# Graph layer with residual and norm on one core: x's part of the update moved behind the products for the edge tables, for seven of thirteen groups instead of three

## The chip, the cores and the metric

The kernel runs on one core of a Trainium2 chip. The metric is the device time of one execution in microseconds; of several runs the median is given.

## The reference

6250 nodes with 128 features each, and 100,000 edges that are sorted by their target node. A message goes through three layers, the messages of a node are averaged, and the node is updated and normalised:

```python
msg_in = jnp.concatenate([x[src], x[dst]], axis=-1)      # 100000 x 256
h = relu(msg_in @ Wm1 + bm1)                             # 256 x 256
h = relu(h @ Wm2 + bm2)                                  # 256 x 256
messages = h @ Wm3 + bm3                                 # 256 x 128
agg = segment_sum(messages, dst) / clip(count, 1)        # 6250 x 128
upd = relu(concatenate([x, agg], -1) @ Wn1 + bn1) @ Wn2 + bn2
out = layernorm(x + (x + upd))
```

## The kernel before

The kernel has three stages. The first works over nodes, in 13 groups of four tiles of 128 nodes (the last group has one tile). For each group it loads x, transposes it on TensorE, and splits the transposed values into a rounded high part (copied by ScalarE, L678) and the rest, the low part (VectorE, L965). With these it computes three products. The product A is x times the upper half of Wm1, and it goes with the bias through `a_out` to the DRAM table `a_table` (L1271 on TensorE, L979 on VectorE, store L508). The product B is x times the lower half of Wm1, and it goes as high part (ScalarE, L662) and low part (VectorE, L989) through `b_out` to `b_table` (store L512). The third product is x's part of the last layer, x times the upper half of Wn1 (`x_product`, L1234); ScalarE copies it with the bias bn1 to `hx` (L669), where it stays until the end. Each of the three takes three terms, high by high, high by low and low by high.

The second stage is the loop over 391 blocks of 256 edges. GpSimd gathers rows of `a_table` by source node (L630), SyncE loads a window of `b_table` (L543) and the target nodes relative to it (`rel`, L546), VectorE makes one-hot matrices (L1023, L1038), TensorE transposes the gathered rows (L1413), adds the expanded window (L1324), computes the second layer (L1437) and sums over the target nodes (L1341 to L1349). ScalarE and VectorE make the high and the low parts of both layers' results (L732, L1106, L740, L1118). The third stage takes the means through the last layers and the norm, group by group.

Each engine has its own program, written out by hand, and they wait for each other by semaphores. In round `g` of the first stage TensorE transposes group `g`, computes the x product that stands first in that round's list `x_groups(g)`, then A of group `g - 1`, then B of the groups `b_groups(g)`, and then the second of `x_groups(g)`, if there is one. B follows one group behind, but B of groups 11 and 12 both stand in the last round, 13. Round 13 also holds the product of Wm3 and the lower half of Wn1 (transposes L1283, copy L865 on VectorE, products L1290 and L1292).

The parts of x lie in seven buffers (`x_parts`, seven being `XB`), which are slices of tensors that the second stage uses: h2_lo, h2_hi, h1, onehot and, for group 6, b_win, the target of SyncE's window loads. wna, the weight of the x product, lies in `onehot_t`. VectorE makes the first `onehot_t` only after `s_bits`, which TensorE's matmul at L1301 raises behind all x products, and after clearing a bank (L1001). `a_out` has two buffers. `b_out` has three, the third of which lies in `a_edge`, where the gathers go; from group 9 on only the first two are used (`b_at`), and a copy into one waits for the store of its last use. The x products use two pairs of banks, (2, 3) and (6, 7); an x product waits for ScalarE's copies of an earlier one:

```python
                if k in X_LAST[1:]:
                    pe.wait_ge(s_hxa, 2 * (x_nth(k) - 2))
                elif k:
                    pe.wait_ge(s_hxa, 2 * (x_nth(k) - 1))
```

In the kernel before, the x products stand as follows: groups 0 and 1 in round 5, 2 in round 6, 3 in round 7, 4 and 5 in round 8, 6 to 9 in rounds 9 to 12 (one each), and 12, 11 and 10 in round 13: the short one of group 12 ahead of L1290, the two others behind it. Ahead of its loop SyncE waits for all stores of both tables and for the words of all blocks (`s_rw`); ScalarE waits for all of its own copies to `hx`.

Of the kernel before, what the change touches and what calls it, by code (L numbers as in the profile page):

```python
# [25 lines left out]
XB = 7  # L26
XA = 5
# [7 lines left out]
def gnn_layer(nc, x, src, dst, Wm1, bm1, Wm2, bm2, Wm3, bm3, Wn1, bn1, Wn2, bn2, out):  # L35
# [13 lines left out]
    NG = -(-NW // GW)  # L49
# [11 lines left out]
    with ExitStack() as ctx:  # L61
# [3 lines left out]
        def sem(name):  # L65
            return ctx.enter_context(nc.semaphore(name))
# [189 lines left out]
        s_hx = sem("s_hx_product")  # L256
# [49 lines left out]
        def size(g):  # L306

            return min(GW, NW - g * GW) if 0 <= g < NG else 0
# [23 lines left out]
            return [NG - 2, NG - 1] if g == NG else [g - 1] if 1 <= g < NG - 1 else []  # L332


        TWICE = (XA, XA + 3)

        def x_groups(g):

            done = max(g - XA, 0) + sum(XA <= t < g for t in TWICE)
            return list(range(done, NG if g == NG else min(done + 1 + (g in TWICE), NG))) if g >= XA else []  # L340

        X_LAST = [NG - 1, NG - 2, NG - 3]
        assert x_groups(NG) == sorted(X_LAST) and all(g >= XB + x for x in range(NG - 3) for g in (XB + x,)
                                                      if x not in x_groups(g))
        X_ORDER = [k for k in range(NG - 3)] + X_LAST

        def x_banks(k):
            return (2, 3) if k == NG - 2 else (6, 7)  # L350

        def x_nth(k):

            return X_ORDER.index(k) + 1

# [6 lines left out]
        def b_uses(k, g):  # L362

            return sum(b_at(j) == k for j in range(g))
# [96 lines left out]
        def _(sp):  # L461
# [43 lines left out]
            for g in range(1, NG + 1):  # L505
                k = g - 1
# [26 lines left out]
            for k in range(3):  # L533
                sp.wait_ge(s_bs[k], 16 * b_uses(k, NG))
            sp.wait_ge(s_rw, 11)

            def body(i):
                first = load_words(sp, words_sp, i * U, U, PAD_DST)
                for k in range(U):
                    if there(i, k - RB):  # L540
                        sp.wait_ge(s_ex, i * U + (k - RB + 1))
                    if there(i, k):
                        sp.dma_start(b_win[:, k % RB, :].bitcast(F32),  # L543
                                     b_table[bass.ds(first[k] * 2, P), :]).then_inc(s_bw[k % RB], 16)
                    if k % 2 == 1:
                        sp.dma_start(rel[:, k // 2, :].rearrange("p (b e) -> p b e", b=2),  # L546
                                     rel_dram[bass.ds(i * U + (k - 1), 2), :].partition_broadcast(P)
                                     ).then_inc(s_rc[k // 2], 16)
# [90 lines left out]
        def _(act):  # L639
# [25 lines left out]
            def copy_hx(k):  # L665
                n = size(k)
                act.wait_ge(s_hx, x_nth(k))
                for h, to in enumerate((hx[0], hx_more)):
                    act.activation(to[:, k * GW * P:(k * GW + n) * P], bank[x_banks(k)[h]][:, 0:n * P],  # L669
                                   ACT.Identity, bias=bn1_col[:, h:h + 1]).then_inc(s_hxa, 1)  # L670

            for g in range(NG + 1):
# [25 lines left out]
                if g < NG:  # L698
                    for k in x_groups(g)[1:2]:
                        copy_hx(k)  # L700
            for k in X_LAST:
                copy_hx(k)
# [499 lines left out]
        def _(pe):  # L1202
# [21 lines left out]
            def x_product(k):  # L1224

                n = size(k)
# [5 lines that stand above are left out]
                for h in range(KH):  # L1232
                    for n_, (xp, a) in enumerate(((0, 0), (0, 1), (1, 0))):
                        ins = pe.matmul(in_pairs(bank[x_banks(k)[h]], n), wna[:, a, h * P:(h + 1) * P], x_part(k, xp),  # L1234
                                        start=(n_ == 0), stop=(n_ == 2))
                ins.then_inc(s_hx, 1)

            for g in range(NG + 1):

                if g == 4:  # L1240
                    pe.wait_ge(s_efs, 1)
                    edge_transposes(0)
                if g == 7:
                    pe.wait_ge(s_hxa, 2 * x_groups(g)[0])
                    pe.wait_ge(s_rel, 1)
                    edge_transposes(1)
                n, k = size(g), g % 2
                if n:
                    pe.wait_ge(s_x[g], 16)
                    if g >= 2:  # L1250
                        pe.wait_ge(s_xl, g - 1)
                    for j in range(n):
                        ins = pe.transpose(bank[k][:, j * P:(j + 1) * P], f_x[:, g * GW + j, :], ident[:, :])
                    ins.then_inc(s_xt, 1)
                if g < NG:
                    for k in x_groups(g)[0:1]:
                        if k == 0:
                            pe.wait_ge(s_wnas, 1)
                            pe.wait_ge(s_ec, GR)
                        if g == 7:  # L1260
                            pe.wait_ge(s_ec, 2 * GR)
                        x_product(k)
                if g == 1:
                    pe.wait_ge(s_split, 1)
                n, k = size(g - 1), g - 1
                if n:
                    pe.wait_ge(s_xl, g)
                for q in range((n + 1) // 2):
                    if k >= 1:
                        pe.wait_ge(s_ac, pair(k - 1, q))  # L1270
                    products(bank[2 + q], k, q, 0).then_inc(s_pa, 1)  # L1271
                for k in b_groups(g):
                    for q in range((size(k) + 1) // 2):
                        if k >= 1:
                            pe.wait_ge(s_bl, pair(k - 1, q))
                        products(bank[4 + q], k, q, 1).then_inc(s_pb, 1)
                if g < NG:
                    for k in x_groups(g)[1:2]:
                        x_product(k)
                if g == NG:  # L1280
                    pe.wait_ge(s_w3, 48)
                    for c in range(KH):
                        ins = pe.transpose(bank[0][:, c * P:(c + 1) * P], w3[:, c, :], ident[:, :])  # L1283
                    ins.then_inc(s_w3t, 1)
                    x_product(X_LAST[0])

                    pe.wait_ge(s_ac, NPAIR)
                    pe.wait_ge(s_w3c, 1)
                    for c in range(KH):
                        pe.matmul(bank[1][:, c * H:(c + 1) * H], w3_t[:, c * P:(c + 1) * P], wn1[:, 1, :],  # L1290
                                  start=True, stop=True)
                    pe.matmul(bank[0][0:2, H:2 * H], b3_col[:, :], wn1[:, 1, :], start=True, stop=True  # L1292
                              ).then_inc(s_wcp, 1)
                    x_product(X_LAST[1])
                    x_product(X_LAST[2])

            pe.wait_ge(s_bl, NPAIR)
            pe.wait_ge(s_const, 8)
# [153 lines left out]
            for g in range(NG + 2):  # L1452
                n, k = size(g), g % 2
# [60 lines left out]
```

## Time and profile before

| | |
|---|---|
| runs | 1200.52, 1201.52, 1202.63 us; median 1201.52 us |
| the profiled execution | 1202.17 us, span from first to last instruction 1200.4 us |
| TensorE | busy 1168.4 us, 97% of the span; mean granted clock 0.992 of full |
| VectorE, ScalarE, GpSimd | busy 966.4, 747.2, 773.9 us |
| first block of the second stage on TensorE | from 89.83 us |

Times in the trace count from the first instruction. In the rows below PE is TensorE's matmul, DVE VectorE, ACT ScalarE, POOL GpSimd, and SPq the instructions by which SyncE issues transfers. A line L1234 is that of the kernel's file. The busy times are no measure of what bounds a stage: matmuls are pipelined, and their ends are modelled. The 1.77 us between the span and the execution's time lie outside the instructions.

### The profile page before, as it was taken

Reading aid. Unit: us, or ns where it says so; the run is one execution under the profiler, and the core shown is the slowest. Engines: PE = TensorE matmul, PEld = TensorE weight load, DVE = VectorE, ACT = ScalarE, POOL = GpSimd, SP = SyncE. Lnnn points to the kernel's source line nnn. Section 1 sums busy time; section 2 is a strip of 40 time slices with the busy share of each in tenths; the row PEclk is TensorE's granted clock in tenths of the full one; section 3 lists DMA queues with packets and bytes.
Section 4 is the critical chain, followed back from the end, with each engine's and each line's share of the span. In section 5 each row is a group of like instructions: output and inputs, shape, how many; then the busy total and the mean of one; then the engine's idle time right before and its main releaser. Section 6 shows DMA issues by size and latency. Waiting matters only on the chain.

```text
span 1200.4 us, 33956 instructions
## 1 busy us (share of the span) xinstructions
PE 1168.4 (97%) x9614; PEld 1147.6 (96%) x9615; DVE 966.4 (81%) x2072; ACT 747.2 (62%) x1392; POOL 773.9 (64%) x814
## 2 busy tenths in 40 slices
PE   6879999999999999999999999999999999999996
PEld 6769999999999999999999999999999999999886
DVE  6766888888777888788888888888888888987676
ACT  3545666666666666666666666666666666664684
POOL 2067777777777777777777777777777777771000
PEclk9999999999999999999999999999999999999998
DMA  9776666666666666665666666666666666662022
GB/s 328 277 284 181 179 179 177 180 179 175 182 180 177 179 178 178 179 183 178 176 178 180 177 181 178 175 179 180 177 181 176 179 176 180 178 178 73 27 71 92
DMA packets 135605, 211.42 MB, mean 176 GB/s; under 512 B 24247, under 2 KB 102669, under 8 KB 134030
## 3 DMA queue, kind: packets, MB, share of 16 engines
q0 software_dynamic: 37536, 102.55, 31.2%
q1 hardware_dynamic: 98030, 108.43, 29.3%
q8 instruction: 14, 0.23, 0.1%
q14 instruction: 25, 0.20, 0.1%
HBM read 188.09 MB, written 22.80 MB: 176 GB/s over the span
## 4 chain that ended last, share of the span: by engine, by line
PE 93%; DVE 2%; SPq 1%; DMA 1%; issue 1%; ACT 1%; POOL 0%; ACTq 0%; DVEq 0%
PE bank L1437 46%; PE bank L1413 14%; PE bank L1324 8%; PE sums L1347 4%; PE sums L1341 4%; PE sums L1345 4%; PE sums L1349 4%; PE bank L1478 3%; PE sums L1491 2%; PE bank L1234 1%; PE bank L1219 1%; PE sums L1219 1%; PE bank L1461 1%; PE bank L1474 0%; PE sums L1462 0%
## 5 line engine op out<-in xcount | busy, mean ns | idle before, releaser
L630 POOL DMA_INDIRECT a_edge<-a_table,src_idx x782 | 754.5, 965 | 255.0 <-issue 176.8
L1437 PE MATMUL bank<-w,h 128*128 128x256 f32 x4692 | 618.8, 281 | 0.0
L1437 PEld LDWEIGHTS bank<-w,h 128*128 128x128 f32 x4692 | 582.5, 189 | 0.0
L732 ACT ACTIVATE h<-bank 128x512 fp32r<-128x512 f32 x391 | 233.9, 598 | 321.2 <-PE bank L1324 319.9
L1106 DVE SCALAR_TENSOR_TENSOR h<-bank,h 128x512 fp32r<-128x512 f32 x391 | 269.3, 689 | 125.3 <-ACT h L732 91.8
L1118 DVE SCALAR_TENSOR_TENSOR h_lo<-bank,h_hi 128x512 fp32r<-128x512 f32 x391 | 266.5, 682 | 0.0
L721 ACT COPY bank<-b_bc 128x512 f32<-128x512 f32 x391 | 231.6, 592 | 46.9 <-DVE h_lo L1118 42.9
L1413 PE MATMUL bank<-ident,a_edge 128*128 128x128 f32 x1564 | 235.8, 273 | 7.0 <-DVE onehot_t L1023 5.6
L740 ACT ACTIVATE h_hi<-bank 128x512 fp32r<-128x512 f32 x391 | 232.9, 596 | 2.9 <-PE bank L1437 2.9
L1324 PE MATMUL bank<-onehot_t,b_win 128*128 128x256 f32 x782 | 189.9, 324 | 0.0
L1413 PEld LDWEIGHTS bank<-ident,a_edge 128*128 128x128 f32 x1564 | 181.2, 140 | 8.1 <-DVE onehot_t L1023 6.7
L1023 DVE TENSOR_SCALAR onehot_t<-rel,node_half 128x256 fp32r<-128x256 int16 x391 | 149.1, 382 | 49.0 <-DMA rel<-rel_dram 36.5
L1038 DVE SCALAR_TENSOR_TENSOR onehot<-iota,first_node,dst_col 128x256 fp32r<-128x256 int16 x391 | 186.1, 476 | 0.5 <-PE sums L1349 0.5
L1324 PEld LDWEIGHTS bank<-onehot_t,b_win 128*128 128x128 f32 x782 | 118.8, 192 | 0.3 <-issue 0.3
L1341 PE MATMUL sums<-h_hi,onehot 128*128 128x258 f32 x391 | 111.0, 284 | 0.2
L1347 PE MATMUL sums<-h_hi,onehot 128*128 128x258 f32 x391 | 111.0, 284 | 0.0
L1345 PE MATMUL sums<-h_lo,onehot 128*128 128x256 f32 x391 | 110.2, 282 | 0.1
L1349 PE MATMUL sums<-h_lo,onehot 128*128 128x256 f32 x391 | 109.9, 281 | 0.0
L1341 PEld LDWEIGHTS sums<-h_hi,onehot 128*128 128x128 f32 x391 | 73.6, 188 | 0.9 <-issue 0.8
L1345 PEld LDWEIGHTS sums<-h_lo,onehot 128*128 128x128 f32 x391 | 74.0, 189 | 0.5 <-issue 0.4
L1347 PEld LDWEIGHTS sums<-h_hi,onehot 128*128 128x128 f32 x391 | 74.1, 189 | 0.0
L1349 PEld LDWEIGHTS sums<-h_lo,onehot 128*128 128x128 f32 x391 | 73.5, 188 | 0.0
(190 smaller groups left out, 681.1 us busy)
## 6 DMA issues: line engine op xcount, KB each, us to landing
b_win<-b_table SPq DMA_DIRECT2D x391, 128.0 KB
rel<-rel_dram SPq DMA_DIRECT2D x196, 128.0 KB, 3.3
a_edge<-a_table,src_idx POOLq DMA_INDIRECT x782
a_table<-work SPq DMA_DIRECT2D x12, 512.0 KB, 4.4
b_table<-work SPq DMA_DIRECT2D x5, 1024.0 KB, 5.7
b_table<-h SPq DMA_DIRECT2D x4, 1024.0 KB, 5.3
f_x<-in_x SPq DMA_DIRECT2D x12, 256.0 KB, 4.5
b_table<-a_edge SPq DMA_DIRECT2D x3, 1024.0 KB, 5.6
```

The source lines that it names most:

```text
L630: pool.indirect_dma_start(a_edge[:, b % R * TB + t, :], None, a_table, bass.IndirectOffsetOnAxis(ap=src_idx[:, b * TB + t:b * TB + t + 1], ...
L721: act.copy(bank[H2[k % U]][:, :], b2_bc[:, :, :].rearrange("p t h -> p (t h)")).then_inc(s_bias, 1)
L732: act.activation(h1[:, k % U, 0, :], bank[k % 2][:, :], ACT.Relu).then_inc(s_h1h, 1)
L740: act.activation(h2_hi[:, (k - LAG) % U, :, 0:H], bank[H2[(k - LAG) % U]][:, :].rearrange("p (t h) -> p t h", t=TB), ACT.Relu).then_inc(s_ ...
L1106: dve.scalar_tensor_tensor(h1[:, k % U, 1, :], bank[k % 2][:, :], 0.0, h1[:, k % U, 0, :].bitcast(F32), ALU.max, ALU.subtract).then_inc(s_ ...
L1118: dve.scalar_tensor_tensor(h2_lo[:, j, :, :], bank[H2[j]][:, :].rearrange("p (t h) -> p t h", t=TB), 0.0, h2_hi[:, j, :, 0:H].bitcast(F32) ...
L1324: ins = pe.matmul(bank[k % 2][:, h * EB:(h + 1) * EB], rows[:, h * P:(h + 1) * P], hot, start=False, stop=True, skip_group_check=True)
L1341: return pe.matmul(to[:, 0:HC], onehot[:, slot, 0, :], h2_hi[:, k % U, 0, :], start=start, stop=False, skip_group_check=True)
L1345: pe.matmul(to[:, 0:H], onehot[:, slot, 0, :], h2_lo[:, k % U, 0, :], start=False, stop=False, skip_group_check=True)
L1347: pe.matmul(to[:, 0:HC], onehot[:, slot, 1, :], h2_hi[:, k % U, 1, :], start=False, stop=False, skip_group_check=True)
L1413: ins = pe.matmul(bank[k % 2][:, h * EB + t * P:h * EB + (t + 1) * P], a_edge[:, k % R * TB + t, h * P:(h + 1) * P], ident[:, :], start=(t ...
L1437: ins = pe.matmul(to, h1[:, j, a, h * EB + t * P:h * EB + (t + 1) * P], w2[:, b, h, :], start=False, stop=(a == 1 and h == KH - 1), skip_g ...
```

## The change

The list of x products is made anew. Groups 0 and 1 stand in round 5 and groups 2 to 5 in rounds 6 to 9, one each; rounds 10 to 12 have none; groups 6 to 12 all stand in round 13, in this order: 6 ahead of L1290, 7 to 12 behind it, on the two pairs of banks in turn. Since the parts of group 6 lie in b_win, SyncE waits for that group's product ahead of its loop.

```diff
-        TWICE = (XA, XA + 3)
+        X_LAST = list(range(NG - XB, NG))
 
         def x_groups(g):
 
-            done = max(g - XA, 0) + sum(XA <= t < g for t in TWICE)
-            return list(range(done, NG if g == NG else min(done + 1 + (g in TWICE), NG))) if g >= XA else []
-
-
-
-        X_LAST = [NG - 1, NG - 2, NG - 3]
-        assert x_groups(NG) == sorted(X_LAST) and all(g >= XB + x for x in range(NG - 3) for g in (XB + x,)
-                                                      if x not in x_groups(g))
-        X_ORDER = [k for k in range(NG - 3)] + X_LAST
+            first = [[0, 1], [2], [3], [4], [5]]
+            return X_LAST if g == NG else first[g - XA] if XA <= g < XA + len(first) else []
+
+        X_ORDER = [k for g in range(NG + 1) for k in x_groups(g)]
+        assert X_ORDER == list(range(NG)) and all(k + XB > g for g in range(NG) for k in x_groups(g))
 
         def x_banks(k):
-            return (2, 3) if k == NG - 2 else (6, 7)
+            return (2, 3) if k in X_LAST[1::2] else (6, 7)
@@ SyncE, ahead of its loop
             sp.wait_ge(s_rw, 11)
+            sp.wait_ge(s_hx, x_nth(max(k for k in range(NG) if k % XB == XB - 1)))
@@ TensorE, at the end of round NG
-                    x_product(X_LAST[1])
-                    x_product(X_LAST[2])
+                    for k in X_LAST[1:]:
+                        x_product(k)
```

## Rows read from the trace of the kernel before

**Rows 1.** The page, busy time of each engine, its share of the span and instructions.

```profile
PE 1168.4 (97%) x9614; PEld 1147.6 (96%) x9615; DVE 966.4 (81%) x2072; ACT 747.2 (62%) x1392; POOL 773.9 (64%) x814
```

**Rows 2.** The chain of waits that ended last: start us, us, what.

```profile
79.28 3.75 DMA b_table<-h
...
109.26 3.00 issue
```

**Rows 3.** Timeline of TensorE: start us, us, instruction, count, [idle before, releaser].

```profile
17.05 2.90 PE L1219 MATMUL bank<-h,h_hi 128*128 128x256 f32 x12 [2.48 <-DVE work L979]
...
30.25 2.90 PE L1234 MATMUL bank<-h_lo,onehot_t 128*128 128x512 f32 x6 [3.35 <-DVE onehot_t L969]
...
46.35 1.66 PE L1234 MATMUL bank<-h_hi,onehot_t 128*128 128x512 f32 x6 [1.59 <-ACT dst_col L646]
...
78.36 0.86 PE L1234 MATMUL bank<-onehot,onehot_t 128*128 128x128 f32 x6
79.73 1.10 PE L1290 MATMUL bank<-work 128*128 128x256 f32 x4 [0.51 <-DVE work L865]
...
81.28 1.65 PE L1234 MATMUL bank<-h,onehot_t 128*128 128x512 f32 x6
...
84.20 0.39 PE L1301 MATMUL sums<-w,ones 128*128 128x512 f32 x1
89.83 1.12 PE L1413 MATMUL bank<-ident,a_edge 128*128 128x128 f32 x4 [5.24 <-DVE onehot_t L1023]
90.60 0.78 PE L1324 MATMUL bank<-onehot_t,b_win 128*128 128x256 f32 x2
...
98.26 0.60 PE L1413 MATMUL bank<-ident,a_edge 128*128 128x128 f32 x4
98.62 0.48 PE L1324 MATMUL bank<-onehot_t,b_win 128*128 128x256 f32 x2
```

**Rows 4.** Timeline of VectorE.

```profile
84.88 0.48 DVE L1001 MEMSET sums<- 128x512 f32 x1 [0.34 <-PE sums L1301]
89.42 0.73 DVE L1023 TENSOR_SCALAR onehot_t<-rel,node_half 128x256 fp32r<-128x256 int16 x2 [4.06 <-DMA rel<-rel_dram]
...
102.04 0.35 DVE L1023 TENSOR_SCALAR onehot_t<-rel,node_half 128x256 fp32r<-128x256 int16 x1 [1.23 <-DMA a_edge<-a_table,src_idx]
```

**Rows 5.** Windows: length; busy us (instructions) of PE, PEld, DVE, ACT, POOL; PEclk, DMA share, GB/s.

```profile
55.00:69.20 14.20, 13.28 (x91) 11.93 (x91) 14.13 (x26) 8.65 (x16) 3.42 (x1) 1.00 0.63 256
65.00:78.00 13.00, 12.15 (x90) 11.26 (x89) 9.95 (x18) 7.43 (x14) 10.89 (x1) 1.00 0.97 394
...
90.00:94.50 4.50, 4.11 (x19) 3.81 (x20) 2.06 (x5) 2.17 (x4) 2.28 (x4) 0.50 0.52 158
96.00:98.00 2.00, 2.00 (x19) 2.00 (x19) 0.35 (x1) 0.95 (x2) 1.39 (x3) 1.00 0.63 210
```

**Rows 6.** Timeline of ScalarE.

```profile
78.42 0.37 ACT L662 CAST h<-sums 128x256 fp32r<-128x256 f32 x1 [0.73 <-PE sums L1219]
...
84.41 0.69 ACT L669 ACTIVATE f_x<-bank,bn_col 128x512 f32<-128x512 f32 x1 [0.16 <-PE bank L1234]
84.99 0.68 ACT L669 ACTIVATE work<-bank,bn_col 128x512 f32<-128x512 f32 x1
86.81 0.59 ACT L721 COPY bank<-b_bc 128x512 f32<-128x512 f32 x1 [1.14 <-issue]
```

**Rows 7.** Timeline of SyncE: issues of A(10)'s and B(10)'s stores.

```profile
71.29 0.33 SPq L508 DMA_DIRECT2D a_table<-work  x1
73.34 0.33 SPq L512 DMA_DIRECT2D b_table<-h  x1
```

**Rows 8.** The same stores, DMA issues 70:72 and 72:75: count, KB, us to landing.

```profile
a_table<-work SPq DMA_DIRECT2D x1, 512.0 KB, 4.3
...
b_table<-h SPq DMA_DIRECT2D x1, 1024.0 KB, 4.7
```

**Rows 9.** Timeline of GpSimd: the gather for block 4.

```profile
91.65 0.94 POOL L630 DMA_INDIRECT a_edge<-a_table,src_idx  x1 [1.61 <-PE bank L1324]
```

## The prediction

> **What bounds the kernel now.** I read the page first: TensorE has 97% of the span as busy time [rows 1], most of it in the loop over edge blocks. The change touches nothing there, so it can only move the moment at which that loop gets going, and all that follows with it. So I read the stretch ahead of it. The chain of waits shows what set its end: the last store of b_table is issued at 79.28 and lands 3.75 us later, at 83.03 [rows 2]; then come SyncE's loads for the first blocks, VectorE waits 4.06 us for rel and makes the first onehot_t at 89.42, and TensorE starts block 0 at 89.83 after 5.24 us of idleness [rows 3, 4]. In that idle time the change has its room.
>
> Why did the last store not leave earlier? The windows give two answers. From 55.0 to 69.2 VectorE is busy 14.13 of 14.20 us: it has its row arithmetic (first words, whole words, flags) besides the copies of A and the low parts of B. From 65 to 78 the DMA engines are at a share of 0.97 and move 394 GB/s [rows 5]. TensorE is busy in both stretches too, but it isn't alone, and the other two keep their work.
>
> **What the change takes away ahead of the stores.** Names: x(k) is the product of x's part for group k; A(k), B(k) are that group's products for the two tables; rounds are the loop's steps. x(0) to x(4) stay where they are. x(5) goes from the end of round 8 to round 9; x(6) to x(9) leave rounds 9 to 12. A full x product costs TensorE 1.46 us (two of them between 81.28 and 84.20 [rows 3]), so 5.8 us leave TensorE before the last B, and on ScalarE four pairs of copies at 1.26 (84.41 to 85.67 [rows 6]). What does this give the stores? Up to 69.2 nothing: VectorE's 14.13 us stay, so the stores of groups 8 and 9 are issued when they were, and TensorE waits instead. After that the issues of A(10), B(10), A(11), B(11) can come one to two us earlier, but they come into a queue that is full. A(10) lands at 71.29 + 4.3 = 75.6, B(10) at 73.34 + 4.7 = 78.0 [rows 7, 8]: 2.4 us for its 1024 KB, 437 GB/s. From there to 83.03 the rest lands, 512 + 128 + 1024 + 256 KB in 5.0 us, 394 GB/s. At 437 throughout it would be 4.5 us. So the end of the stores can gain about 0.5 us, and no more as long as the queue decides.
>
> There is a second tie. From group 9 on B has two staging buffers (`b_at`), so ScalarE's copy of B(12) waits for the store of B(10). It ran at 78.42 [rows 6], 0.4 us after that store landed at 78.0. It can therefore come at 78.05, a gain of 0.37. VectorE's low part and its copy of w3's transpose follow in order, and TensorE's w3 product (L1290) starts 1.31 us after ScalarE's copy (78.42 to 79.73 [rows 3, 6]): 79.36 now. B(12) itself doesn't bind here: VectorE's copy of A(12), which stands ahead of the low parts of B(11) in its program, waits for the store of A(10), landed at 75.6; then the two low parts of B(11) (0.69 us each at most, an estimate from ScalarE's copies of that shape [rows 6]), and B(12) is done by 77.3. x(6) fits between B(12) and L1290: 77.4 to 78.9 with the two transposes of w3.
>
> **What the change puts behind.** Behind L1290 stood x(11) and x(10); now there stand x(7) to x(11) and the short x(12), which before ran ahead of L1290. The first starts 1.55 us after L1290 (79.73 to 81.28). Their pace: TensorE could do 1.46, but with two pairs of banks a product waits for the copies of the one two before it; a product's row is 1.65 us, and the pair of copies behind it is 1.26, so two products can't follow in less than 2.91, and each semaphore between the engines adds a little. I take 1.50 each; the bounds are 1.46 (TensorE alone) and 1.65 (the whole row of one product, no overlap at all between neighbours). x(12) costs 0.8, from its row of 0.86 less its overlap with the next. So the marker matmul L1301, which all of VectorE's loop waits for, starts at 79.36 + 1.55 + 5 x 1.50 + 0.8 = 89.2, against 84.20: 5.0 later. VectorE had waited 4.06 us for rel after the memset that this matmul releases. That cover is used up: rel, if it follows the stores, lands 0.5 earlier, at 88.9, while the memset now ends at 90.4. So the first onehot_t is 5.0 - 4.06 = 0.95 later, and TensorE starts block 0 at 90.8, not 89.83.
>
> **What the start gives back.** After its 5.24 us of idleness TensorE ran the first steps at a granted clock of 0.50 from 90.0 to 94.5, that is 1.2 GHz, and at 1.00, 2.4 GHz, from 96 to 98 [rows 5]. Block 0, transposes and expansion, took from 89.83 to 91.38, 1.55 us; block 4 at full clock from 98.26 to 99.10, 0.84 [rows 3]. Now TensorE works until 89.6 and idles some 1.2 us. Idleness of 1.59 us before 46.35 left an x product at 1.66 us, of 3.35 us before 30.25 made it 2.90, and of 2.48 us before 17.05 left twelve A products at 2.90 [rows 3], so at 1.2 us I take the full clock. Block 0 is then expanded at 90.8 + 0.84 = 91.6, against 91.38: 0.2 later. This is the moment that counts, because GpSimd's gather for block 4 waits for it (91.65 after 1.61 idle [rows 9]) and from there gathers follow without a gap, and VectorE waits for them until block 6 and later (1.23 us at 102.04 [rows 4]).
>
> ScalarE is later by more. Its last copies end near 90.6, and 1.14 us of issue stand between them and put_b2, as at 86.81 [rows 6]; so its first relu comes near 92.2, not 91.4, and block 2's transposes with it 0.8 later. Two blocks at half clock with the first h2 product had taken TensorE some 1.2 us more than at full clock, so by block 3 this is paid back. The new wait of SyncE for x(6), near 79, stands behind its wait for the last store, past 82, and costs nothing; behind it stand only the loads of b_win. ScalarE's own waits and GpSimd's queue keep their order; nothing is moved past them, and no DMA is added or dropped.
>
> **The sum** is +0.2 us: 0.37 gained at the stores, 5.38 us of work put behind L1290, 4.06 of cover, 0.7 back at the clock. Against the profiled execution's 1202.17 (span 1200.4) it is 1202.4; the median of the runs, 1201.52, lies 0.65 below that execution, so I say 1201.7. Bounds of the terms: stores -0.5 to +0.3, pace of five products -0.2 to +0.75, clock 0 to +0.7.
>
> **Rivals.**
> (a) *The stores land sooner.* If a store's time were its own and not the queue's, B(10), issued near 71.7 instead of 73.34, would land at 75.5 in the 3.75 us of the last store [rows 2], which had little behind it; then B(12) on TensorE binds, 77.3, L1290 comes at 78.6, and the sum is -0.55: 1201.0. For it: the issues do come earlier. Against it: the landings follow each other at the queue's rate. The Trainium skill (DMA: Bandwidth & Descriptors, Anatomy of one DMA) gives a DMA about 2.0 us plus its bytes at 436 GB/s, which for this store would be an estimated 4.4 us and a landing at 76.1, much as in this rival. By it the sum would be -0.55 too. The trace doesn't agree for this store, which took 4.7 us [rows 8]; by that row the sum stays at +0.2.
> (b) *The loop still starts at 1.2 GHz*, since the first steps have waits between them (1.2 us ahead of block 0, then for the late relu): the 0.7 isn't given back, +0.9: 1202.4. For it: from 90 to 94.5 the clock stayed low though TensorE was busy 4.11 of 4.50 us.
> (c) *Slower: TensorE drops to 1.2 GHz ahead of the tail.* With x(6) to x(9) gone it waits for VectorE and for stores between 60 and 77, by my estimate up to 2.9 us in round 10 (the two products that leave rounds 9 and 10, 2 x 1.46) and up to 2 us ahead of B(12), which waits until the store of A(10) has landed at 75.6. Idleness of 2.48 us was enough at 17.05, of 1.59 was not at 46.35. If it falls ahead of B(12), x(6) takes 2.9 us [rows 3] instead of 1.5, and B(12) and the transposes, by the same ratio, 0.5 more; L1290 comes 1.85 later, and the sum is +2.05; if the loop's start is slow as well, +2.75: 1204.3. It decides from a fall that costs x(6) and block 0 together. A fall in round 10 alone costs nothing, since VectorE is behind then.
> (d) *Faster by more*: the 3.00 us of issue at 109.26 in the chain [rows 2], ScalarE's on entering the loop, goes when ScalarE comes there from other waits. Nothing in the rows ties it to the change; -3: 1198.7.
>
> **How the numbers follow.** The sum as it stands 55%, (a) 14%, (b) 13%, (c) 12%, (d) 6%. A measurement of this kernel can tell about 0.2%, 2.4 us, from no change. The first three cases lie within that; half of (c) and a rest of unforeseen costs lie above it, (d) and a rest of unforeseen gains below: faster 0.09, same 0.75, slower 0.16. The runs shown lie 2.1 us apart, so a median can be off by 1. The likeliest case's own range is 1200.5 to 1203.2; with the bounds of the terms and most of (c), 1199.4 to 1204.6.
>
> **What would show it.** Right: in the changed profile VectorE stays full from 55 to 69 and the stores land back to back, the last near 82.5; L1290 near 79.4, five long x products behind it at 1.5, L1301 near 89.2; VectorE's first onehot_t waits for TensorE and not for rel; block 0 begins near 90.8 at granted clock 1.00. Wrong: the last store landing before 81.5, products at over 1.7, a granted clock of 0.5 in the tail, or ScalarE's first relu, not the gathers, setting the pace beyond block 4.

## The result, and the profile after

The changed kernel takes 1203.62 us (median of 20 runs, 1201.26 to 1205.86), the kernel before 1202.12 us in as many runs beside it (1200.03 to 1204.57). The ratio is 1.0013, its 95% interval 1.0007 to 1.0019: 0.8 to 2.3 us slower, 1.5 in the middle. The prediction had said +0.2 us and "same" by a bound of 0.2%, and a range that holds the time; the sign of its sum was right, its size was not. That the sign came out right says little, since by its own bounds for the terms the sum could also have been below zero. Where the other 1.3 us come from is the question of this study.

The profiled execution took 1205.11 us with a span of 1203.3. Its page, busy time of each engine, answers to [rows 1]:

```profile
PE 1168.0 (97%) x9614; PEld 1147.2 (95%) x9615; DVE 960.7 (80%) x2072; ACT 748.3 (62%) x1392; POOL 772.1 (64%) x814
```

The sums of work are as they were; only the order moved. What lies ahead of the change shifts everything behind it by up to 2.4 us from profile to profile, so times are counted from one instruction that the change doesn't reach: VectorE's operation over the words of all blocks. VectorE works without a gap for 8.2 us up to it, in before (from 50.82) as in after (from 52.20). In the profile of before and in that of after (timeline of VectorE) it stands at

```profile
59.04 0.55 DVE L925 CUSTOM_DVE_ANT_0 words_pe<-words_pe,agg 1x784 uint16<-1x784 uint16 x1
```

```profile
60.41 0.55 DVE L922 CUSTOM_DVE_ANT_0 words_pe<-words_pe,agg 1x784 uint16<-1x784 uint16 x1
```

so 1.37 is subtracted from a time of after to compare it with one of before. Of these 1.37 us 1.1 arise in round 5, ahead of the change, where the two profiles run the same instructions. TensorE's granted clock from 30 to 38 us was 0.79 in before and 0.59 in after, and the twelve products of an A and of a B took longer; first before's, then after's:

```profile
32.95 1.95 PE L1219 MATMUL bank<-h 128*128 128x256 f32 x12
34.74 1.60 PE L1219 MATMUL sums<-h 128*128 128x256 f32 x12
```

```profile
33.27 2.76 PE L1216 MATMUL bank<-h 128*128 128x256 f32 x12
35.83 1.89 PE L1216 MATMUL sums<-h 128*128 128x256 f32 x12
```

Times counted from the words operation leave this out, but the time of an execution holds it. Lines of after are 3 or 4 lower: L1287 is before's L1290, L1298 its L1301, L1020 its L1023. TensorE's timeline of after, answering to [rows 3]:

```profile
64.81 2.90 PE L1216 MATMUL bank<-h,h_hi 128*128 128x256 f32 x12 [2.98 <-DVE work L976]
...
78.82 0.63 PE L1216 MATMUL sums<-h,onehot 128*128 128x256 f32 x3 [0.69 <-DVE work L986]
79.28 0.38 PE L1280 MATMUL bank<-ident,work 128*128 128x128 f32 x2
79.42 1.63 PE L1231 MATMUL bank<-b_win,onehot_t 128*128 128x512 f32 x6
80.89 1.02 PE L1287 MATMUL bank<-work 128*128 128x256 f32 x4
...
82.36 3.03 PE L1231 MATMUL bank<-h_lo,onehot_t 128*128 128x512 f32 x12
85.37 3.06 PE L1231 MATMUL bank<-h_hi,onehot_t 128*128 128x512 f32 x12
88.40 1.66 PE L1231 MATMUL bank<-h,onehot_t 128*128 128x512 f32 x6
89.90 0.78 PE L1231 MATMUL bank<-onehot,onehot_t 128*128 128x128 f32 x6
90.52 0.44 PE L1298 MATMUL sums<-w,ones 128*128 128x512 f32 x1
92.75 0.66 PE L1410 MATMUL bank<-ident,a_edge 128*128 128x128 f32 x4 [1.79 <-DVE onehot_t L1020]
93.17 0.48 PE L1321 MATMUL bank<-onehot_t,b_win 128*128 128x256 f32 x2
```

The reader is to see the moved products there: x(6) at 79.42, x(7) to x(11) from 82.36 to 89.90 at 1.5 us each, x(12), and the marker matmul at 90.52, which is 89.15 in before's time (89.2 was predicted). VectorE, answering to [rows 4], and the chain of waits in that place, which shows what VectorE's sequencer does between its two instructions:

```profile
91.25 0.48 DVE L998 MEMSET sums<- 128x512 f32 x1 [5.52 <-PE sums L1298]
92.34 0.61 DVE L1020 TENSOR_SCALAR onehot_t<-rel,node_half 128x256 fp32r<-128x256 int16 x2 [0.61 <-issue]
```

```profile
82.44 8.25 PE bank L1231 x36
90.68 0.29 PE sums L1298
...
91.60 0.59 DVEq L418
...
92.34 0.36 DVE onehot_t L1020
...
92.75 0.33 PE bank L1410
...
113.48 2.92 issue
```

From round 10 to block 0 no DMA stands in this chain. The wait of 4.06 us for rel is gone, but 0.61 us of "issue" remain between the memset and the first onehot_t: mostly L418, VectorE's loads of the first blocks' words into registers. Before, they ran under the wait for rel and no row showed them. The last line is the 3 us of issue on entering the loop [rows 2], still there, now found on VectorE.

GpSimd's gather for block 4, answering to [rows 9], and the windows, answering to [rows 5] (the last one, 64 to 66, is new):

```profile
93.92 0.95 POOL L627 DMA_INDIRECT a_edge<-a_table,src_idx  x1 [2.37 <-PE bank L1321]
```

```profile
55.00:69.20 14.20, 11.22 (x75) 10.75 (x74) 13.65 (x26) 5.16 (x10) 2.04 (x1) 0.81 0.64 259
65.00:78.00 13.00, 12.25 (x80) 12.00 (x80) 10.17 (x18) 3.65 (x7) 10.84 (x1) 0.78 0.85 343
90.00:94.50 4.50, 2.54 (x20) 2.02 (x18) 1.28 (x4) 3.19 (x7) 1.83 (x3) 1.00 0.52 164
96.00:98.00 2.00, 2.00 (x19) 2.00 (x19) 0.96 (x3) 0.60 (x1) 1.39 (x3) 1.00 0.62 195
64.00:66.00 2.00, 1.19 (x5) 1.22 (x6) 2.00 (x5) 0.00 (x0) 0.00 (x0) 0.50 0.00 0
```

The first two show that VectorE stays full up to 69 (13.65 of 14.20 us) while TensorE falls behind it, and that the DMA engines are less full from 65 to 78 than in before (0.85 and not 0.97). The last shows that TensorE's clock is at 0.50 (1.2 GHz) around the products that follow the idleness of 2.98 us in round 10. The third shows the loop's start at 1.00 (2.4 GHz), where before had 0.50.

Counted from the words operation, the steps stand like this (a subtraction of rows, 59.04 and 60.41):

| | before | after | difference |
|---|---|---|---|
| w3 product (L1290, now L1287) | 20.69 | 20.48 | -0.21 |
| marker matmul (L1301, now L1298) | 25.16 | 30.11 | +4.95 |
| block 0 on TensorE | 30.79 | 32.34 | +1.55 |
| gather for block 4 | 32.61 | 33.51 | +0.90 |

### The profile page after: what moved, and what is told of

It reads as the page before. It is cut to its first block, busy times and chain, and to the rows that moved or that the text cites. A ratio compares the mean times of both kernels' runs of the same rounds, so it can differ in the third digit from the quotient of the medians.

```text
span 1203.3 us, 33956 instructions
## 1 busy us (share of the span) xinstructions
PE 1168.0 (97%) x9614; PEld 1147.2 (95%) x9615; DVE 960.7 (80%) x2072; ACT 748.3 (62%) x1392; POOL 772.1 (64%) x814
## 4 chain that ended last, share of the span: by engine, by line
PE 93%; DVE 3%; DMA 1%; issue 1%; POOL 1%; ACT 0%; SPq 0%; DVEq 0%
PE bank L1434 45%; PE bank L1410 14%; PE bank L1321 8%; PE sums L1344 4%; PE sums L1338 4%; PE sums L1342 4%; PE sums L1346 4%; PE bank L1475 3%; PE sums L1488 2%; PE bank L1231 1%; PE bank L1458 1%; PE bank L1216 1%; PE sums L1216 1%; POOL a_edge L627 1%; PE bank L1471 0%
## 5 line engine op out<-in xcount | busy, mean ns | idle before, releaser
L1020 DVE TENSOR_SCALAR onehot_t<-rel,node_half 128x256 fp32r<-128x256 int16 x391 | 144.1, 369 | 54.0 <-DMA rel<-rel_dram 40.7
```

## The experiments

The expectations use letters. **T**: the start of the loop is held by the products behind L1287, less what VectorE's wait for rel had covered, and the gathers of the first blocks carry the delay on. **C**: the cost is the clock's fall in round 10. **F**: the rounds ahead of L1287, from which x products were taken, give back or cost a part of it. **Q**: the last stores are bound by a full DMA queue. **L**: the loads behind the last stores still hold the start. Each kernel was timed in five rounds, beside the kernel before on the same chip.

**One part of the cover taken away in the kernel before** (`e1_rel_three`): SyncE loads rel for the first blocks ahead of its wait for the last stores.

```diff
@@ SyncE, ahead of the wait for the stores; the loop then skips these loads for i = 0
+            sp.wait_ge(s_rw, 11)
+            first_of_0 = load_words(sp, words_sp, 0, U, PAD_DST)
+            for c in range(RC):
+                load_rel(2 * c, c)
```

> The kernel before, with SyncE's loads of rel for the first four blocks, and its registers for their windows, ahead of its wait for the last stores. Theory T (ahead of the change the start of the edge loop was set by the loads that follow the last store, which cover TensorE's tail; the change puts 5.4 us of x products behind L1290 and uses that cover up): block 0 on TensorE starts near 87 instead of 89.8, and from there GpSimd's gathers, which idled 1.6 us ahead of block 4, hold it: 1.0 to 1.6 us faster than before. If the loads behind the last store held nothing, no change.

1201.76 us against 1202.36, ratio 0.9998 (0.9988 to 1.0008). Block 0 came at 29.55 behind the words operation, 1.24 earlier than in before, and the gather for block 4 at 32.19, 0.42 earlier. The 1.0 to 1.6 us that were expected did not come, and no gain is shown. Block 0 did not come near 87 either: with rel there, VectorE's first onehot_t waits for another load behind the stores, SyncE's window of b_table, which has to stay behind them, since it reads what they write:

```profile
88.53 0.57 DVE L1030 TENSOR_SCALAR onehot_t<-rel,node_half 128x256 fp32r<-128x256 int16 x1 [2.18 <-DMA b_win<-b_table]
```

What else holds the gather for block 4 a kernel below shows.

**The same in the changed kernel** (`e2_rel_seven`).

> The changed kernel with the same two moves on SyncE. Theory T: TensorE's tail holds the start, so earlier loads give nothing: 1.0 to 2.0 us slower than the kernel before, as the changed kernel is, and VectorE's first onehot_t comes behind L1298 as there. Rival L (the loads behind the last stores still hold the start, and the changed kernel's loss is elsewhere): it gains 1 us or more over the changed kernel.

1203.86 us, ratio 1.0010 (1.0001 to 1.0019); block 0 at 32.53. With seven groups behind, the loads are not what block 0 waits for. This profile bears on C as well: behind the same 2.98 us of idleness in round 10 the clock stayed at 1.00 from 64 to 66, and block 0 came as late as in after.

```profile
64.53 1.66 PE L1223 MATMUL bank<-h,h_hi 128*128 128x256 f32 x12 [2.98 <-DVE work L983]
```

**The tail cut short** (`e3_short_tail`): in the changed kernel only the high by high term is computed for groups 7 to 12; the two other terms are left out.

```diff
-                    for n_, (xp, a) in enumerate(((0, 0), (0, 1), (1, 0))):
+                    terms = ((0, 0),) if k > X_LAST[0] else ((0, 0), (0, 1), (1, 0))
+                    for n_, (xp, a) in enumerate(terms):
```

> The changed kernel with one term of three (high by high) in the x products of groups 7 to 12: two thirds of that product's work are left out. Theory T: the tail shrinks to ScalarE's pace of 1.26 us a group, L1298 comes some 2 us earlier than in the changed kernel, the loads of rel hold the start again, and the time is within 0.5 us of the kernel before. Rival C (the cost is the drop of TensorE to 1.2 GHz in round 10, and the late B(9)): it stays 1.0 to 2.0 us slower than before.

1201.85 us, ratio 1.0001 (0.9993 to 1.0010): the cost is gone, while all other instructions of the change, those of rounds 9 to 12 included, are in place. The clock did not fall in round 10 in this profile, so it alone doesn't speak against C; it fell in the tail instead, to 0.50 from 86 to 88. VectorE's timeline:

```profile
88.37 0.48 DVE L998 MEMSET sums<- 128x512 f32 x1 [3.63 <-PE sums L1299]
89.46 0.61 DVE L1020 TENSOR_SCALAR onehot_t<-rel,node_half 128x256 fp32r<-128x256 int16 x2 [0.61 <-DMA rel<-rel_dram]
```

The trace names rel here as what ended the wait, but onehot_t follows the memset by the same 0.61 us as in after: that is the least they stand apart.

**Five and six groups behind** (`e7_five`, `e8_six`): in the changed kernel groups 6 and 7, or 6 alone, go back to rounds 10 and 11.

```diff
-        X_LAST = list(range(NG - XB, NG))
+        X_LAST = list(range(NG - 5, NG))       # e8: NG - 6
-            first = [[0, 1], [2], [3], [4], [5]]
+            first = [[0, 1], [2], [3], [4], [5], [6], [7]]      # e8: without [7]
```

> Five products behind (groups 8 to 12; 6 and 7 go back to rounds 10 and 11), so three full ones and the short one behind L1290 instead of five and the short one. Theory T: the tail ends before the loads behind the last store, which set the start again: within 0.5 us of the kernel before, VectorE's first onehot_t waits for a DMA. Rival C (TensorE's idleness in front is what costs): between the two kernels, about 0.8 us slower than before.

> Six products behind (groups 7 to 12; 6 goes back to round 10): four full ones and the short one behind L1290. Theory T: the tail and the loads end within 0.5 us of each other, block 0 starts up to 0.5 us later than in the kernel before but at the full clock, so -0.5 to +0.7 us. Rival C: about 1.2 us slower than before.

1201.71 us (1.0001, 0.9992 to 1.0010) and 1202.61 us (1.0004, 0.9995 to 1.0013). Block 0 is at 30.31 and 32.28. With five behind the cover holds: the first onehot_t still waits 1.29 us for rel. With six it doesn't in this profile, but the tail was not all that came late there. TensorE's clock fell ahead of it, behind 1.58 and 1.88 us of idleness:

```profile
78.00:82.00 4.00, 4.00 (x14) 2.38 (x12) 1.08 (x4) 1.64 (x3) 1.13 (x1) 0.61 0.87 350
```

The marker matmul came 30.04 behind the words operation, no earlier than in after with one product more (30.11). With after's rows behind the w3 product and four long products in place of five, an estimate for block 0 is 30.9, beside 30.79 in before. So six stand at the edge of the cover, and its time is not shown to be above before's.

**The clock kept up** (`e4_warm`): ten dummy matmuls into a bank that is free then, in round 10 of the changed kernel.

```diff
+                if g == 10:
+                    pe.wait_ge(s_hxa, 2 * x_nth(5))
+                    for _ in range(10):
+                        pe.matmul(bank[6][:, :], wab[:, 0, 0:P], wab[:, 0, :], start=True, stop=True)
```

> The changed kernel with ten extra matmuls of 512 columns into a free bank in round 10, in the gap of 3 us in which TensorE waits for VectorE; their result isn't used. Theory T: the clock stays at 2.4 GHz, the store of B(9) is issued 1 to 1.6 us earlier, but the stores land as before in the changed kernel, and the time stays 1.0 to 2.0 us slower than the kernel before. Rival C: the loss goes, within 0.5 us of the kernel before.

1205.42 us (7 runs), ratio 1.0027 (1.0016 to 1.0038). TensorE's timeline shows that the dummies did what they were for, since A(9) takes 1.67 us and not 2.90:

```profile
61.79 2.54 PE L1265 MATMUL bank<-h 128*128 128x512 f32 x10
65.02 1.67 PE L1216 MATMUL bank<-h,h_hi 128*128 128x256 f32 x12 [0.68 <-DVE work L976]
```

The w3 product didn't come sooner for it (20.61 behind the words operation, 20.48 in after), and the time is no shorter. With e2, where the clock stayed up without dummies and block 0 came no sooner, C is excluded as the cost. That this kernel is slower than the changed one was not expected; it was run again below.

**The tail without the rest of the change** (`e5_twice_three`): the kernel before, with the products of groups 7 to 10 computed a second time behind the three, into the sum banks that the memset clears; their results are not used.

```diff
@@ TensorE, behind x_product(X_LAST[2])
+                    pe.wait_ge(s_bl, NPAIR)
+                    for k in (7, 8, 9, 10):
+                        for h in range(KH):
+                            for n_, (xp, a) in enumerate(((0, 0), (0, 1), (1, 0))):
+                                pe.matmul(in_pairs(bank[SUM + h], GW), wna[:, a, h * P:(h + 1) * P], x_part(k, xp),
+                                          start=(n_ == 0), stop=(n_ == 2))
```

> The kernel before with four x products (groups 7 to 10) computed once more behind the last one, into the two sum banks, where nothing reads them: the tail of the changed kernel with nothing taken away in front. Theory T: 5.8 us on TensorE against a cover of 3.4 us (4.06 us of waiting less VectorE's 0.6 us of register loads, which the wait had hidden): block 0 starts 2.4 us later but at the full clock, and the time is 1.4 to 2.4 us above the kernel before, hardly more than in the changed kernel, since moving the products gave the stores only 0.2 to 0.4 us. Rival F (the moved products do free the front, and the tail costs more than the net shows): 3 us or more above the kernel before.

1205.47 us against 1201.83, ratio 1.0028 (1.0018 to 1.0038). That the tail alone makes before slower is shown, but +3.4 us is above T's bound and in F's. By place it isn't F: the w3 product starts at 20.70 here, as in before (20.69), and in the changed kernel at 20.48 in one profile and 20.80 in another, so taking the products away ahead of it gained nothing there. Block 0 at 32.88 is 0.54 later than in after, and 0.16 later than in the second profile of the changed kernel. What the rest of +3.4 is stays open.

**VectorE's register loads moved ahead** (`e6_setup_seven`): in the changed kernel they stand ahead of the wait for the marker matmul.

```diff
-            dve.wait_ge(s_bits, 1)
-            dve.memset(bank[SUM][:, :], 0.0).then_inc(s_sz, 1)
@@ behind VectorE's other preparations for the loop
+            words_of_0 = load_words(dve, words_dve, 0, words_of(0, BACK + 2), DVE_TOP)
+            dve.wait_ge(s_bits, 1)
+            dve.memset(bank[SUM][:, :], 0.0).then_inc(s_sz, 1)
```

> The changed kernel with VectorE's register setup and its loads of the first words ahead of its wait for TensorE's marker matmul L1298. Theory T: VectorE's first onehot_t follows its memset at once, block 0 starts 0.6 to 0.9 us earlier than in the changed kernel, and the time is 0.3 to 1.2 us above the kernel before. If that setup isn't on the path, no change from the changed kernel, 1.0 to 2.0 us above.

1204.17 us, ratio 1.0016 (1.0007 to 1.0025). The 0.6 us are real: VectorE's onehot_t follows its memset at once, and block 0 and the gather for block 4 come 0.71 earlier than in after (31.63 and 32.80). The time didn't follow: it was expected at 0.3 to 1.2 us above before, and a gain of 0.7 on the changed kernel is neither shown nor excluded by intervals of this width. In this profile TensorE's clock fell behind block 2 instead:

```profile
91.05 0.48 DVE L1012 MEMSET sums<- 128x512 f32 x1 [5.36 <-PE sums L1300]
91.44 0.54 DVE L1021 TENSOR_SCALAR onehot_t<-rel,node_half 128x256 fp32r<-128x256 int16 x2
```

```profile
95.32 0.66 PE L1412 MATMUL bank<-ident,a_edge 128*128 128x128 f32 x4 [1.94 <-DVE onehot_t L1021]
95.73 0.48 PE L1323 MATMUL bank<-onehot_t,b_win 128*128 128x256 f32 x2
96.05 2.36 PE L1436 MATMUL bank<-w,h 128*128 128x256 f32 x12
98.21 1.05 PE L1412 MATMUL bank<-ident,a_edge 128*128 128x128 f32 x4
```

**Both covers taken away in the kernel before** (`e9_rel_setup_three`): the edits of the first and of the last experiment together, with three groups behind.

> The kernel before (three groups behind) with both covers taken away: SyncE issues the first five loads of rel ahead of its wait for the last stores, and VectorE loads the first words into registers ahead of its wait for the marker matmul. Theory T (the start is held by the last marker matmul, then by the gathers of the fill, which run on GpSimd from the landing of the last store of a_table): block 0 comes 1.0 to 1.8 us earlier than before, but the gather of block 4 only 0.0 to 0.4 us earlier, counted from the words operation; the time is 0.3 to 1.2 us below before. If GpSimd's chain of gathers is the whole limit, the time is within 0.5 us of before, as with the loads of rel alone (-0.6).

1200.68 us against 1202.01, ratio 0.9994 (0.9985 to 1.0003): the lowest median of the study, but not shown to be faster. Block 0 is at 29.09, 1.70 earlier than in before, the gather for block 4 at 31.70, 0.91 earlier, more than expected. The chain of waits shows the next limit:

```profile
76.42 3.46 DMA a_table<-work
79.89 0.52 issue
80.41 1.13 POOL a_edge L637
...
89.54 0.95 POOL a_edge L637
90.48 0.30 issue
90.79 0.95 POOL a_edge L637
```

From the landing of a_table's last store GpSimd issues the gathers of the first blocks, most of them 1.25 us apart, and the one for block 4 (90.79) comes 10.38 us behind the first (80.41) without a gap. In before that distance was 11.50 (80.15 to 91.65), in after 12.44 (81.48 to 93.92), with the first loads of rel alone 10.39 (81.40 to 91.79). So, with a_table's last store landing when it does, 1.1 us is all that an earlier start could give to before, and these gathers are the floor under it. Block 0 itself is still held by a load here, as in the first experiment: its onehot_t waits 1.68 us for the window of b_table.

**Half the bytes in three stores** (`e10_half_stores`): in the changed kernel the stores of B for groups 8 to 10 write the high part only; the low parts of these rows are written as zeros in round 7, so this part is left out of the result.

```diff
@@ SyncE, store of B(k)
+                    if 8 <= k <= 10:
+                        sp.dma_start(<high parts of the rows of group k>,
+                                     b_out[b_at(k)][:, 0:GW, 0, :].bitcast(F32)).then_inc(s_bs[b_at(k)], 16)
+                        continue
@@ SyncE, round 7
+                    for j in (8, 9, 10):
+                        sp.dma_start(<low parts of the rows of group j>, <zeros>).then_inc(s_bz, 16)
```

> The changed kernel, with the stores of B for groups 8 to 10 cut to their high part; the low parts of these rows are written as zeros by three transfers in round 7, so that part is left out of the result. Theory Q (the last copies of h wait for stores that are themselves bound by a full queue): B(10)'s store lands 1 us or more earlier, B(12)'s copy is then bound by TensorE, the w3 product starts up to 0.9 us earlier and the time is 0.5 to 1.0 us below the changed kernel run beside it. If the queue is not the limit there, the w3 product starts where it did and the time is that of the changed kernel, +1.0 to +2.0 us against before.

**The changed kernel again, and the warm one again** (`e11_seven_again`, `e12_warm_again`), on the same chip.

> The changed kernel itself once more, as the measure for its three neighbours: +0.8 to +2.3 us against before by every theory, w3 product to block 0 about 11.9 us, block 0 about 32.3 us behind the words operation.

> The changed kernel with ten dummy matmuls in round 10 (the kernel of e4_warm), beside the changed kernel itself. If the clock in round 10 costs nothing (theory T) and the dummies cost nothing, it is within 0.7 us of the changed kernel run beside it; if the dummies themselves delay the stores or the copies, it is 1 us or more above it, as +3.3 us against before in the run of e4_warm suggests; if the lower clock were the cost (rival C), it would be 1 us or more below it.

Half the stores: 1201.57 us against 1202.01, ratio 1.0000 (0.9991 to 1.0009), 2.2 below the changed kernel beside it by the medians, where 0.5 to 1.0 were expected. The changed kernel again: 1203.76, 1.0015 (1.0006 to 1.0023), as in its first measurement. The warm one: 1204.91, 1.0022 (1.0012 to 1.0031), 1.2 above the changed kernel, with intervals that overlap.

Q holds in part. The store of B(10), in the DMA issues of the changed kernel, the warm one and the one with half the bytes (KB, us from issue to landing):

```profile
b_table<-h SPq DMA_DIRECT2D x1, 1024.0 KB, 4.2
```

```profile
b_table<-h SPq DMA_DIRECT2D x1, 1024.0 KB, 7.0
```

```profile
b_table<-h SPq DMA_DIRECT2D x1, 512.0 KB, 3.2
```

It was issued at 75.19, 72.11 and 73.12, which is 14.78, 12.51 and 13.70 behind the words operation; it landed 19.0, 19.5 and 16.9 behind it. Issued 2.3 us earlier, the same store landed 0.5 later. In all thirteen profiles with the full stores it is issued between 12.5 and 14.9 us behind the words operation and lands between 19.0 and 19.7: an earlier issue gave nothing. With half the bytes it landed 2.6 us sooner than in the warm kernel, though issued 1.2 later; against after it was issued 1.1 earlier and took 1.0 less. The w3 product came at 19.39 and block 0 at 31.25, 1.1 us earlier than in after, and the cost of the change was gone from the time. In the profile of after the store is not the limit: its queue had run low (DMA share 0.42 from 70.4 to 72.4), the stores came late behind the fall in round 10, and ScalarE's copy of B(12) waited for TensorE. In e2, without the fall, that copy waited 2.58 us for the store of B(10). Both ways end at nearly the same w3 product (20.48 and 20.59).

All of it side by side (us behind the words operation in the one profile of each kernel; ratio to before):

| kernel | w3 product | block 0 | gather for block 4 | ratio |
|---|---|---|---|---|
| e9, three behind, no covers | 20.70 | 29.09 | 31.70 | 0.9994 |
| e1, three behind, rel early | 21.11 | 29.55 | 32.19 | 0.9998 |
| e7, five behind | 20.58 | 30.31 | 32.13 | 1.0001 |
| before, three behind | 20.69 | 30.79 | 32.61 | 1 |
| e3, short tail | 20.69 | 30.81 | 32.62 | 1.0001 |
| e10, half stores | 19.39 | 31.25 | 32.41 | 1.0000 |
| e6, registers early | 20.55 | 31.63 | 32.80 | 1.0016 |
| e8, six behind (clock low in the tail) | 20.62 | 32.28 | 33.45 | 1.0004 |
| after, seven behind | 20.48 | 32.34 | 33.51 | 1.0013 |
| e2, rel early | 20.59 | 32.53 | 33.70 | 1.0010 |
| e4, warm | 20.61 | 32.56 | 33.86 | 1.0027 |
| e11, after again | 20.80 | 32.72 | 33.89 | 1.0015 |
| e12, warm again | 20.94 | 32.88 | 34.05 | 1.0022 |
| e5, tail alone | 20.70 | 32.88 | 34.06 | 1.0028 |

All kernels with the gather for block 4 up to 32.62 are within 0.06% of before, and those with it from 33.45 on are 0.04 to 0.28% above it, whatever brought it there; of these e8, at 0.04%, is not shown to be slower. e6 alone stands out.

## Why the prediction was right, and its size wrong

**What bounds the change** was right: it acts through the loop's start alone. The short tail, which keeps the rest of the change, takes the cost away, so does the tail of five groups, and the tail alone in the kernel before brings one.

**The tail.** 5.38 us were to be added behind L1290: the first product 1.55 after it, five more at 1.50, x(12) at 0.8. Measured from L1287 to the marker matmul it is 9.63 (80.89 to 90.52) against 4.47 before (79.73 to 84.20): 5.16. The pace of 1.50 was right; the short x(12) took 0.62 (89.90 to 90.52) and not 0.8.

**The cover** is the step that failed: "That cover is used up ... So the first onehot_t is 5.0 - 4.06 = 0.95 later." The 4.06 of [rows 4] is not all cover: 0.61 of it VectorE needs in any case, for its registers, and a wait that ends later hides whatever the engine does ahead of it. What the change could use up was 4.06 - 0.61 = 3.45. VectorE's row of after shows 0.61 of "issue" once rel is no longer late, the short tail shows the same 0.61, and moving the register loads ahead brought block 0 forward by 0.71. That is shown by place; in the time of e6 it is not shown. The prediction had counted such a pause for ScalarE, 1.14 us of issue, but none for VectorE.

**The stores.** 0.37 was to be gained. The w3 product came 0.21 earlier in one profile of the changed kernel and 0.11 later in the other; among the kernels with the full stores it lies between 20.48 and 21.11. By the mean of the two profiles the gain is nothing, to some tenths. The reason given for the bound, "they come into a queue that is full", was right for the profiles without a fall in round 10, and more strictly than the sum had it. In after, where TensorE fell to 1.2 GHz in round 10, the issue of B(10) came 0.5 later than in before and not one to two us earlier.

**The start at full clock.** 0.7 was to be given back. From block 0 to the gather for block 4 before took 1.82 us (89.83 to 91.65), after 1.17 (92.75 to 93.92): 0.65. The granted clock is 1.00 in the window 90 to 94.5.

With these sizes the sum is 5.16 - 3.45 - 0.65 - 0.0 = +1.1 us in place of +0.2, which lies in the measured interval of 0.8 to 2.3; the gather for block 4 is 0.90 later in one profile and 1.28 in the other. The predicted 90.8 for block 0 was 91.4 in before's time, for the 0.61. The 1.2 us of idleness foreseen ahead of it were 1.79.

**The rivals.** (a), stores that land sooner because a store's time is its own, is refuted by e2 and e12, where B(10) was issued 1.8 us earlier than in before and took 6.7 and 7.0 us for the same bytes. The Trainium skill (DMA: Bandwidth & Descriptors, Anatomy of one DMA), whose section speaks of transfers issued from GpSimd, gives an estimated 4.4 us for a transfer of that size. Of these stores, issued by SyncE, after's came near it with 4.2, behind a stretch in which the queue had run low; those into a full queue did not. (b), a loop that starts at 1.2 GHz, was not so in the two profiles of the changed kernel. But the fall can come later: in the warm kernel's second profile the windows show it,

```profile
94.00:100.00 6.00, 5.31 (x25) 5.02 (x25) 2.95 (x6) 2.11 (x5) 4.48 (x6) 0.50 0.62 177
```

and not in its first, where the same stretch is at 1.00. (c), the fall ahead of the tail, came in the changed kernel in round 10 alone (ahead of the tail it came in e8), and "A fall in round 10 alone costs nothing" was right: without it (e2, e4, e12) the stores of B(10) land no sooner, and the chain runs over them; with it the chain runs over TensorE, and both end at the same w3 product. (d) can't be read from one profile. The stall of issue on entering the loop, 3.00 us in before's chain and 2.92 in after's, is there in the changed kernel's second profile too, 2.66 us on ScalarE, and in e9 with 2.92. But the chain of the second profile runs over TensorE there, with less:

```profile
111.50 1.27 issue
```

From the words operation to the last instruction that execution took 1141.6 us, the first of the same kernel 1142.9 and before's 1141.4. So this stall goes and comes from execution to execution of one kernel, and nothing ties it to the change, as the prediction said.

**What stays open.** The three kernels with matmuls added (e4, e12, e5) are 1.2 to 1.9 us slower than the changed kernel by their medians, though the intervals of their ratios overlap its interval and their block 0 lies at most 0.5 later than in after. e6 started 0.7 earlier and didn't become faster; its clock fell in the profiled execution, and whether it does in most is not known. From the words operation to block 12 single profiles differ by more than the medians do, since a gather of one of the first blocks sometimes lands late: the one in the chain took 3.73 us in before and 5.32, 5.01 and 5.12 in after, e5 and e12, but 4.05 in e11. A rival for part of the time lies ahead of the change: the longer stretch at 1.2 GHz in round 5, worth 1.1 us, stands in both profiles of the changed kernel (clock 0.59 and 0.57 from 30 to 38) and in those of e2 and e4 (0.61 and 0.58), while before and eight others have 0.79 and e9 1.00. The instructions there are the same in all, and how often it comes in executions without a profile is not known. So the profiles bear out the place of the cost, and the tenths of the +1.5 that are above +1.1 are not explained.

## What to carry to other kernels

A wait that the profile shows is cover only down to what its engine has to do anyway before its next instruction; before a wait is counted as room, look at what the program holds between the two instructions, register loads included, for these don't show while the wait is longer. Where stores at the end of a stage fill the DMA queue, ask whether an earlier issue can make them land earlier: here it didn't over 2.4 us of issue times, and work taken away ahead of them gave nothing, while half the bytes moved their end. Where a stage's tail is the room for moved work, its size is a number of pieces: five groups fitted, six stood at the edge, seven didn't fit. And one profile of a kernel is one draw: the clock fell in different places in executions of the same instructions, so a place is believed when several profiles show it.

## What the runs showed of the hardware

The same 1024 KB store took 4.2 to 7.0 us; wherever in a stretch of 2.4 us it was issued, it landed within 0.7 us of the same place. TensorE's clock didn't always fall after the same idleness: behind 2.98 us in round 10 the twelve A products took 2.90 us in both profiles of the changed kernel (granted clock 0.50 from 64 to 66 in after), but 1.67 in the kernel with the short tail, where the clock stayed at 1.00 up to 68 with the same instructions up to there:

```profile
63.45 1.67 PE L1216 MATMUL bank<-h,h_hi 128*128 128x256 f32 x12 [2.98 <-DVE work L976]
```

Nor after shorter idleness: with 1.58 and 1.88 us of it ahead of the tail the clock fell in e8 (0.61 from 78 to 82), with 1.57 and 1.87 us it stayed at 1.00 in e4.
